# Two heads' masks on ScalarE, and the transposed x kept in device memory

## The reference

```python
# layer 1: linear attention, 16 heads of 16, 64 features each
qp = relu(q @ rw) + EPS;  kp = relu(k @ rw) + EPS        # q, k, v = x W + b
kv = einsum('bhsf,bhsd->bhfd', kp, v)                     # over the whole sequence
out = (qp @ kv) / (qp . sum(kp) + EPS);  x = layernorm(x + out @ Wo + bo)
# layer 2: gated MLP plus experts picked by product keys (4 heads, 64 x 16 of 64 x 64 pairs exist)
sx, sy = top 8 scores of the two halves of the query, per head
scores = top 8 of the 64 sums sx[i] + sy[j];  w = silu(x . down[idx]) * softmax(scores)
x = layernorm(x + silu(x Wg + bg) * (x Wu + bu) @ Wd + bd + sum(w * up[idx]))
```

## Time and profile before

| | us |
|---|---|
| median of 3 runs (lowest, highest) | 3860.46 (3854.98, 3862.65) |
| the profiled execution's own time | 3858.18 |
| its span, first to last instruction | 3856.4 |
| TensorE busy | 3674.8 (95%) |
| VectorE busy | 3076.9 (80%) |
| GpSimd busy | 1675.2 (43%) |
| ScalarE busy | 1339.8 (35%) |

### The profile page before, as it was taken

One profiled execution on the slowest core, in us unless ns is written; L12 is line 12 of the kernel. 1 busy time (PEld: TensorE's weight loads), 2 busy tenths in 40 slices (PEclk: granted clock), 3 DMA queues, 4 the chain that ended last, 5 costly groups with the idle time before them and its releaser, 6 DMA issues. The chain is left out here.

```text
span 3856.4 us, 51959 instructions
## 1 busy us (share of the span) xinstructions
PE 3674.8 (95%) x19388; PEld 3095.6 (80%) x19388; DVE 3076.9 (80%) x5947; ACT 1339.8 (35%) x1990; POOL 1675.2 (43%) x1004
## 2 busy tenths in 40 slices
PE   8969999999999999999999999999999999999988
PEld 7758888888788888888888887888888888777766
DVE  2388888888788878888878888888888888999983
ACT  3323333333333333333333333333333333333321
POOL 0144444444444444454444454444444444555541
PEclk8769999999999999999999999999999999999999
DMA  3000000000000000000000000000000000000000
GB/s 111 17 12 6 12 17 17 17 12 12 12 18 17 17 12 12 15 14 17 17 12 12 17 12 17 17 12 12 17 12 17 17 6 12 12 11 12 6 6 12
DMA packets 23337, 61.15 MB, mean 16 GB/s; under 512 B 5552, under 2 KB 10032, under 8 KB 23088
## 3 DMA queue, kind: packets, MB, share of 16 engines
q1 hardware_dynamic: 18480, 41.04, 3.4%
q0 software_dynamic: 4608, 16.78, 1.1%
HBM read 41.04 MB, written 16.78 MB: 15 GB/s over the span
## 5 line engine op out<-in xcount | busy, mean ns | idle before, releaser
L430 POOL TENSOR_TENSOR grid<-ex 128x1024 f32<-128x1024 f32 x512 | 1245.6, 2440 | 626.3 <-ACT ex L812 286.7
L1020 DVE SCALAR_TENSOR_TENSOR grid<-grid,best 128x1024 f32<-128x1024 f32 x512 | 736.8, 1439 | 31.0 <-POOL grid L430 30.2
L1036 DVE SCALAR_TENSOR_TENSOR prob<-grid,rz,prob 128x1024 f32<-128x1024 f32 x384 | 694.6, 1809 | 3.4
L687 PE MATMUL y_bank<-wd_sb,gate 128*128 128x256 f32 x2048 | 625.2, 387 | 15.6 <-DVE wexp L1058 15.6
L689 PE MATMUL y_bank<-up_sb,wexp 128*128 128x256 f32 x2048 | 612.3, 381 | 0.0
L595 PE MATMUL ring<-x1T_hl,downT_hl 128*128 128x512 f32 x1536 | 417.5, 407 | 19.0 <-ACT gate L817 19.0
L689 PEld LDWEIGHTS y_bank<-up_sb,wexp 128*128 128x128 f32 x2048 | 391.7, 191 | 54.0
L595 PE MATMUL ring<-x1T_hl,wg_hl 128*128 128x512 f32 x1536 | 423.6, 411 | 7.9 <-DVE gate L1052 7.7
L595 PE MATMUL ring<-x1T_hl,wu_hl 128*128 128x512 f32 x1536 | 418.0, 407 | 0.0
L421 POOL TENSOR_SCALAR qp<-qp 128x512 f32<-128x512 f32 x256 | 217.0, 848 | 432.4 <-ACT qp L803 421.0
L687 PEld LDWEIGHTS y_bank<-wd_sb,gate 128*128 128x128 f32 x2048 | 355.9, 192 | 58.3 <-issue 29.9
(11 more groups left out here) (146 smaller groups left out, 5693.2 us busy)
## 6 DMA issues: line engine op xcount, KB each, us to landing
xb<-in_L_attn_x SPq DMA_DIRECT2D x34, 512.0 KB, 3.5
out_y<-x POOLq DMA_DIRECT2D x32, 512.0 KB, 3.1
xa<-in_L_attn_x SPq DMA_DIRECT2D x30, 512.0 KB, 3.4
prob<-in_L_ffn_down_embed SPq DMA_DIRECT2D x1, 1024.0 KB, 5.9
prob<-in_L_ffn_Wg SPq DMA_DIRECT2D x1, 1024.0 KB, 8.7
prob<-in_L_ffn_Wu SPq DMA_DIRECT2D x1, 1024.0 KB, 10.5
wd_sb<-in_L_ffn_Wd SPq DMA_DIRECT2D x1, 1024.0 KB, 11.4
up_sb<-in_L_ffn_up_embed SPq DMA_DIRECT2D x1, 1024.0 KB, 12.0
```

The source lines that it names most:

```text
L430: pool.tensor_tensor(grid[:, h % 2], bcast(ex[:, h, 0:NX].unsqueeze(2), [P, NX, NK]), bcast(ex[:, RH + h, 0:NK].unsqueeze(1), [P, NX, NK]) ...
L687: pe.matmul(rows, gate[:, c % 2, t * P:(t + 1) * P], wd_sb[:, c, :], start=(c == 0 and t % 2 == 0), stop=False, skip_group_check=True)
L1020: marks["keep", h] = rt_steps.mark(dve.scalar_tensor_tensor(out=g, in0=g, scalar=best[:, h, TOP - 1:TOP], in1=g, op0=ALU.is_ge, op1=ALU.mult))
L1036: ins = dve.scalar_tensor_tensor(out=row, in0=g, scalar=rz[:, h:h + 1], in1=row, op0=ALU.mult, op1=ALU.add, accum_out=mass[:, 0:1] if h == ...
```

## The change

Two things.

First, the kv stage's `xaT` is written to device memory (`xT_kept`) by a DMA from SyncE's queue, and the at stage reads it into `xbT` by a DMA four iterations later. The two "turn" parts leave AT_SEQ, with their eight transpositions on TensorE and two copies on ScalarE; the other at parts keep their places. The load into `xbT` is issued when TensorE has done wo 1 of the group before. GpSimd's bias add (L416, now L440) no longer waits for "turn 1"; it waits only for the load of `xb`.

Second, heads 0 and 1 are masked by ScalarE in place of VectorE. With b the eighth best and r the scale, a parametric ReLU of (g - b) with slope 2^30 below zero makes everything under the threshold hugely negative, and a ReLU of r times that plus r b gives r g above the threshold and 0 below. VectorE makes -b ("drop") and r b ("lift") for both heads. For head 0 the result goes straight into `prob`, for head 1 back into the grid; VectorE adds the two by one `tensor_tensor` (add 1). keep 0, keep 1 and add 0 are gone from VectorE. Spread 2 now waits for head 0's second ScalarE instruction; VectorE's add 1 stands directly before add 2, behind wexp.

```diff
-    AT_SEQ = ([("turn", 0), ("turn", 1), ("q", 0), ("q", 1)] + [("qp", j) for j in range(4)] + [("qkv", 0)]
+    AT_SEQ = ([("q", 0), ("q", 1)] + [("qp", j) for j in range(4)] + [("qkv", 0)]
...
             def body(it, par, kv, at, rt, ff, last, batch):      # SyncE
...
                     if m == 0:
-                        sp.wait_ge(*full("kv", 2 * FILL - 1, "turn", 1))
+                        sp.wait_ge(*full("kv", 2 * FILL - 1, "sum", T - 1))
+                        sp.wait_ge(xbT_kept, FILL * 16)
                     else:
+                        sp.wait_ge(*full("at", m - 1, "wo", 1))
+                    lane, i = in_lane(m)
+                    sp.wait_ge(lane.kept, (i + 1) * 16)
+                    sp.dma_start(xbT, xT_kept[m]).then_inc(xbT_loaded, 16)
+                    if m:
                         sp.wait_ge(*drained("at", m - 1, "wo", 1))
                     sp.dma_start(xb[:], x_groups[m]).then_inc(xb_loaded, 16)
+                if kv:
+                    keep(a)                       # wait for both turns drained, then xT_kept[a] <- xaT
...
                     pool.wait_ge(xb_loaded, (m + 1) * 16)
-                    pool.wait_ge(*full("at", m, "turn", 1))
                     pool.tensor_tensor(xb[:], xb[:], bcast(bo_sb[:].unsqueeze(1), [P, T, D]),
...
-                    wait(pool, rt_dve, s * RT_STEPS + (t - (h < 2)) * len(RT_TILE) + RT_AT["add", (h - 2) % RH])
+                    if h == 2:
+                        pool.wait_ge(masked, s * (ACT_HEADS * T) + t * ACT_HEADS + 1)
+                    else:
+                        wait(pool, rt_dve, s * RT_STEPS + (t - (h < 2)) * len(RT_TILE) + RT_AT["add", (h - 2) % RH])
...
+                def mask(t, h):                   # ScalarE
+
+                    act.wait_ge(spread_ready, s * (RH * T) + t * RH + h + 1)
+                    act.wait_ge(rt_dve, s * RT_STEPS + t * len(RT_TILE) + RT_AT["lift"])
+                    g = grid[:, h].rearrange("p a b -> p (a b)")
+                    act.activation(g, g, ACT.Prelu, bias=drop[:, h:h + 1], alpha=STEEP).then_inc(bent, 1)
...
+                    act.wait_ge(bent, s * (ACT_HEADS * T) + t * ACT_HEADS + h + 1)
+                    act.activation(prob[:, other, t, :] if h == 0 else g, g, ACT.Relu, scale=rz[:, h:h + 1],
+                                   bias=lift[:, h:h + 1]).then_inc(masked, 1)
...
+                    if rt and c % 2:
+                        mask(c // 2, 0)
...
+                    rt_steps.mark(dve.tensor_scalar(drop[:], best[:, 0:ACT_HEADS, TOP - 1], -1.0, None, ALU.mult))
...
+                    rt_steps.mark(dve.tensor_tensor(lift[:], best[:, 0:ACT_HEADS, TOP - 1], rz[:, 0:ACT_HEADS],
+                                                    ALU.mult))
...
-                        ins = dve.tensor_scalar(row, g, rz[:, 0:1], None, ALU.mult)
+                    if h < ACT_HEADS:
+
+                        dve.wait_ge(masked, s * (ACT_HEADS * T) + t * ACT_HEADS + ACT_HEADS)
+                        ins = dve.tensor_tensor(row, g, row, ALU.add)
...
                     if rt and odd:
-                        add_head(t, 2)
+                        add_head(t, 1), add_head(t, 2)
```

More of the change, by code:

```diff
@@ L168, in block_kernel @@
         AT_STEPS = 2 * T + 2 * T
-        RT_TILE = (["top", "less", "cand", "best", "sum", "rz"]
-                   + [(step, h) for h in range(RH) for step in ("keep", "add")] + ["mass"])
+        RT_TILE = ["top", "less", "cand", "best", "drop", "sum", "rz", "lift", ("keep", 2), ("add", 1),
+                   ("add", 2), ("keep", 3), ("add", 3), "mass"]
         RT_AT = {name: k + 1 for k, name in enumerate(RT_TILE)}
@@ L173, in block_kernel @@
         Y_STEPS = 2 * T
[L176 to L179, removed]
+        at_places = [(c, place) for c in range(C - 1) for place in range(3)][2:len(AT_SEQ)]
+        at_place = {at: [use] for at, use in zip(at_places, AT_SEQ)}
+        AT_EARLY, AT_MID, AT_LATE = ([at_place.get((c, place), []) for c in range(C)] for place in range(3))
+        AT_LATE[C - 1] = AT_SEQ[-2:]
+        assert len(at_places) == AT_USES - 2 and at_place[6, 1] == [("wo", 1)]
         kv_places = [(c, place) for c in range(C) for place in range(3) if place or c >= C - 2]
@@ L359, in _, with keep @@
                 load(dst[:], src.partition_broadcast(P))
-            for r in range(1, FILL):
-                for k, lane in enumerate(LANES):
-                    sp.wait_ge(*full("kv", 2 * (r - 1) + k, "turn", 1))
-                    sp.dma_start(lane.x[:], x_groups[2 * r + k]).then_inc(lane.loaded, 16)
+            def keep(a):
+                lane, i = in_lane(a)
+                sp.wait_ge(*drained("kv", a, "turn", 0))
+                sp.wait_ge(*drained("kv", a, "turn", 1))
+                sp.dma_start(xT_kept[a], lane.xT[:]).then_inc(lane.kept, 16)
+            for r in range(FILL):
+                for k, lane in enumerate(LANES):
+                    if r:
+                        sp.wait_ge(*full("kv", 2 * (r - 1) + k, "turn", 1))
+                        sp.dma_start(lane.x[:], x_groups[2 * r + k]).then_inc(lane.loaded, 16)
+                for k in range(2):
+                    keep(2 * r + k)
             def body(it, par, kv, at, rt, ff, last, batch):
@@ L837, in body @@
                         ff_dots(c)
+                    if rt and c % 2:
+                        mask(c // 2, 1)
                     if at:
@@ L1129, in body @@
                         add_head(t, 3), clamp(t)
-                    if rt and not odd:
-                        keep(t, 0)
-                    if rt and not odd and c:
-                        add_head(t, 0)
                 assert not rt or rt_steps.k == RT_STEPS
```

53 lines of the change are left out of this document (22 added, 31 removed).

## The result

The changed kernel takes 3892.56 us (median of 4 runs, 3890.68 to 3896.79), the kernel before, beside it, 3860.99 (3854.98 to 3862.65). The ratio is 1.0086, with a 95% interval of 1.0069 to 1.0104: slower by 32 us, where the prediction had 3845 and a range to 3886. The profiled execution's span is 3891.7 us, its mean granted clock 0.969 (before: 3856.4 and 0.978).

The account below looks back on a forecast made before the run. TensorE bounds full iterations, busy 112.1 of 114.8 us. Terms +1.3 (full iterations) - 14 - 5.8 - 4.4 + 1 + 7 (clock) = -15, from 3858.2 to 3843, 3845 as median; range 3780 to 3886.

Parts of the forecast that it names:

- Second transposition: Full iterations: removing it gains TensorE 0.43 us, not 0.87, as q 0 waits 1.68 for its bank in place of 1.25.
- The wait for kT goes: Full iterations, before v 0: masks on ScalarE end TensorE's 1.42 us wait, with 0.9 of slack.
- The rival of longer masks: ScalarE masks longer or later than 2.42 us: 3866 with 0.8 more, 3890 or above with 1.6 more; chance 0.18.
- A new wait at norm 1 of 1.9: Full iterations, step 7: masks' chain, spread 3 and bias add delay norm 1, so TensorE loses 1.9 us.
- Norm 1 isn't held up: Rival: bias add comes later or norm 1 goes through in one go, iterations of 113.0 us, 3787; chance 0.20.
- The granted clock: Full iterations: six more falls of TensorE's clock behind waits, 1.7 us each, 10 in all, 7 taken.
- the clock: Rival: clock falls in every one of 26 full iterations, +44 us in place of 7, 3882; chance 0.12.
- Iterations 32 to 35: Four iterations without kv: waits for h and wexp go, norm 1's partly replaces them; gain of 14 us, between 9.2 and 22.2.
- Iteration 36: Routing without at: a tile's chain takes 20.2 us in place of 21.64, 5.8 gained over four tiles.
- Start: Up to iteration 6: 4.4 us gained in iteration 5, 1 lost as q 0 of group 0 waits for its load.

Follow-up runs that it names:

- e1: Kernel before with only the kept transposition ("turn" removed, bias add early), all four masks on VectorE; 3889.17 us.
- e3: Changed kernel with GpSimd's bias add waiting until TensorE has done the second kv transposition (pt 0 where there is none); 3810.43 us.
- e4: Changed kernel with six filler matmuls on TensorE before it waits for norm 1; 3859.79 us.
- e8: Changed kernel with GpSimd's spread of head 1 issued only when VectorE's lift is done; 3844.42 us.
- e13: Changed kernel with one filler matmul on TensorE before it waits for norm 1; 3863.16 us.
- e5: Changed kernel with norm 1 moved on VectorE ahead of keep 2, bias add still early; 3783.20 us.
- e11: Kernel before with masks on ScalarE, "turn" left in, and the same three order edits as e10; 3724.04 us.
- e10: Changed kernel with norm 1 ahead of keep 2, first scores ahead of the second norm's sums and h, spread 1 behind lift; 3716.44 us.
- e6: Changed kernel with the PSUM banks of q 0 and q 1 exchanged; 3854.51 us.
- e2: Kernel before with only the masks of heads 0 and 1 on ScalarE, "turn" left in, bias add behind it; 3830.77 us.
- e7: Changed kernel with bias add behind the second kv transposition, norm 1 ahead of keep 2, banks of q 0 and q 1 exchanged; 3827.38 us.

## Why the prediction was wrong

Step by step, as it was put:

- **Second transposition**, "q 0 wants this bank ... a wait of 1.25 + 0.43 = 1.68": measured 1.70, and 2.66 at starts (2.65 foreseen). Right.
- **The wait for kT goes**: right. The masks last 1.146 and 1.242 us in place of 1.137 and 1.228, add 1 1.229 in place of 1.25. The rival of longer masks is out. (One addition was short: add 1 at 30.2, a qp addition of 0.62 and add 2 of 1.28 make 32.1 and not 31.8, a slack of 0.5 and not 0.9. It was enough.)
- **A new wait at norm 1 of 1.9**: 1.94 in nearly every full iteration, its cause shown by e1 and e3. The way there was a little different: the sum had add 2 to 113.8 and then spread 3 to 115.55, in the trace spread 3 runs first and add 2 takes 3.03. The two orders end at about the same time, so the 1.9 came out; this part is luck. The net of waits and work in full iterations, +1.3, measured 24.2 - 22.6 = +1.6. "Norm 1 isn't held up" is out. Of the block itself the rows agree only roughly: 1.63 = 0.55 + 1.08 has L1020 finish in 1.08 behind the other, where alone it takes 1.28, so some 0.2 of it wasn't held up.
- **The granted clock: this term failed.** "I count two more, and four of the twenty with 1.7 and 1.9": 6 further falls, 10 us, of which 7 were taken. It was 17, 29 us. Of the 17, 14 are behind norm 1 and 3 at starts of sequences. The mechanism and the price of one, 1.7, were right; the count wasn't. The shortest wait behind which the earlier trace rows showed a fall was 2.2 us, and the four of twenty had no row behind them: between 1.44 and 2.2 the trace of before has a single wait, of 1.52, without a fall (and 44 up to 1.44, where the prediction counts 46). The trace of after shows how narrow it is: 1.70 never, 1.94 in 14 of 26. e4, e8 and e13 show that the time without work is what counts: at 0.47, 1.63 or 1.83 the same wait had no fall. Which of the waits of 1.94 bring one stays open. So the rival "the clock", given 0.12, was the course of the full iterations, with 17 further falls for its 26, well past the 9 from which it said it decides. The 29 in place of 7 would alone have made 3845 + 22 = 3867; the next two terms, 20 and 7, take the time past 3886, the end of the range. The Trainium skill, page TensorE: Matmul & The Clock Gate, section "HAM oscillation — how this bites in real kernels", tells of a loop with a wait in each pass in which TensorE starts slow again each time; the waits there are for DMA and longer than the 1.94 here. The falls behind norm 1 are that pattern, in about every other pass.
- **Iterations 32 to 35, "I take 14"**: +6.3. The wait for wexp (13.0) shrank to 2.7 and that for h to 0.3, but TensorE waits for norm 1 5.54 three times and 3.52 once, 20.1 in all, where I had let 8 come back, and 4.5 more for ScalarE's gate. In the fourth no bias add follows, and e3 has 3.52 in all four: 2.0 is the bias add, 3.5 the chain behind which norm 1 stands. Three more us are falls of the clock (7 in place of 5). So the step that failed was the price of norm 1's wait in these four, put at 8 and measured at 20.1. e5, norm 1 out of the chain, brings the four to 400.1, 20 less.
- **Iteration 36, "20.2"**: 22.25. The sum had the mask behind spread 0. It waits for lift as well, which spread 1 blocks, 2.1 later: 20.2 + 2.1 = 22.3. e8 takes 1.4 of it away and gets 20.9. The Trainium skill, page SBUF — State Buffer, section "SBUF: two separate sides", names the case, a VectorE operation with two SBUF inputs that finds a GpSimd operation running and is blocked until it ends. The rows agree: lift ends at 3755.56, when the two spreads do (3755.54), and takes 1.52 against 0.16. The prediction had used this rule for large operations and left out the smallest one, on which the path hung.
- **Start**: -3.4 foreseen, -3.8 measured.

The forecast of -15 missed the span's +35.3 by 50: 22 in the clock of the full iterations, 20 in iterations 32 to 35, 7 in iteration 36, and 2 at the end. The cause of these 2 stays open. From 272 to 3720 us the clock lost 46.8 us in the changed kernel and 14.0 in the one before, so that without falls the two would be about equal.

## What to carry to other kernels

Before an instruction leaves one engine, list every neighbour that it kept apart: the removed transposition also held the bias add off norm 1, and one wait that does this again was worth 82 us (e3). Count waits not only by their sum but by their length one by one, and where a new wait is near one that already made the clock fall, let the range take in a fall in every pass; here it was 14 of 26. A saving on the bound engine in a loop with waits is worth little until the order on the other engines is mended: the kept transposition, with the bias add that it lets go early, cost 28 us by itself in the old order (e1) and gained 8 in the new one (e11 to e10), while three changes of order, with no work saved, gained 176.

## What the runs showed of the hardware

- TensorE's granted clock fell behind waits of 1.94 us (14 of 26 in the changed kernel, 11 of 26 in e6) and not behind 1.83 (e8, 0 of 26), 1.70 (0 of 19) or 1.63 (e13, 0 of 26); at 2.2 twice in six before and five times in six in e2, at 2.66 once to five times in six, by kernel, at 3.1 to 3.3 in 15 of 18 in e7. Each count is of one execution. Each fall went to 1.2 GHz and cost 1.7 us, in e4 and e8 sometimes twice that behind one wait.
- One filler matmul of 512 columns in a wait shortened the time without work from 1.94 to 1.63 us and took 29 us off the kernel, 24 of it by the 14 falls (e13).
- A two-column VectorE product took 0.16 us free (e8) and 1.52 behind the start of a GpSimd spread (iteration 36).
